# Routing a mixture of experts in two halves: the first among the last causal heads, the second behind the first weighted sums

## The reference

```python
h = _rms(x, n1_w)                                # causal attention, 16 heads of 16
attn = softmax(where(causal, rms(q) @ rms(k).T / 4, -inf))
x = x + (attn @ v @ wo.T with channels 0..63 set to 0)
xf = _rms(x, n2_w)
logits = nan_to_num(xf @ gate_w.T)               # 4 experts
probs = softmax(logits)
topv, topi = top_k(probs, 2)
topv = topv / (topv.sum(-1) + 1e-8)
wts = zeros.at[token, topi].add(topv)
o0 = gelu(xf @ e0_up.T) @ e0_down.T
o1 = silu(xf @ e1_w1.T) * (xf @ e1_w2.T) @ e1_down.T
o2 = gelu(gelu(gelu(xf @ e2_l1.T) @ e2_l2.T) @ e2_l3.T) @ e2_l4.T
o3 = gelu(gelu(xf @ e3_down.T) @ e3_up.T) @ e3_out.T
x = x + (sum of wts[:, e] * oe with channels 0..63 set to 0)
x = layernorm(x)
```

## Time and profile before

| | |
|---|---|
| runs of the kernel, us | 1109.04, 1127.35, 1121.53 |
| median, us | 1121.53 |
| the profiled execution, us | 1125.14 |
| its span, us | 1123.30 |
| its mean granted clock of PE | 0.934 |
| PE busy | 968.8 us (86%) |
| DVE busy | 676.0 us (60%) |
| ACT busy | 591.4 us (53%) |
| POOL busy | 291.2 us (26%) |

### The profile page before, as it was taken

One profiled execution on the slowest core, in us unless ns is written; L12 is line 12 of the kernel. 1 busy time (PEld: TensorE's weight loads), 2 busy tenths in 40 slices (PEclk: granted clock), 3 DMA queues, 4 the chain that ended last, 5 costly groups with the idle time before them and its releaser, 6 DMA issues.

```text
span 1123.3 us, 22133 instructions
## 1 busy us (share of the span) xinstructions
PE 968.8 (86%) x8864; PEld 700.9 (62%) x8864; DVE 676.0 (60%) x1576; ACT 591.4 (53%) x1390; POOL 291.2 (26%) x305
## 2 busy tenths in 40 slices
PE   7997878888779998999898688888888888978997
PEld 4664556666458885566666556666666566645755
DVE  3346545455849965656566477766767766539302
ACT  4632556444348965454554355455546545567444
POOL 3521332000240005212112131221221222337344
PEclk9997899769889999999999899999899899989999
DMA  9350545400668977452252243313213202100001
GB/s 317 106 92 22 122 109 81 116 12 1 204 208 309 315 262 257 151 175 88 96 180 97 71 129 112 104 35 121 77 62 112 56 1 99 71 1 1 1 1 33
DMA packets 66679, 123.72 MB, mean 110 GB/s; under 512 B 11632, under 2 KB 41968, under 8 KB 62496
## 3 DMA queue, kind: packets, MB, share of 16 engines
q1 hardware_dynamic: 64528, 117.48, 34.4%
q0 software_dynamic: 2048, 4.82, 1.4%
HBM read 86.30 MB, written 35.92 MB: 109 GB/s over the span
## 4 chain that ended last, share of the span: by engine, by line
PE 52%; DVE 22%; ACT 12%; DMA 6%; issue 4%; POOL 3%; SPq 1%; POOLq 0%; DVEq 0%; ACTq 0%
PE psum L413 36%; ACT s_p L2803 4%; DVE s_p L2845 3%; DVE s_max L2834 2%; DMA raw_wd<-in_wd 2%; PE psum L2762 2%; PE psum L2773 2%; PE psum L1410 2%; DVE s_pT L2826 1%; PE psum L2236 1%; DVE junk L1930 1%; PE psum L2946 1%; PE psum L568 1%; DVE s_max L687 1%; DMA ctx_raw<-in_ctxT 1%
## 5 line engine op out<-in xcount | busy, mean ns | idle before, releaser
L2803 ACT ACTIVATE s_p<-psum,s_max 112x375 f32<-112x375 f32 x128 | 72.1, 568 | 98.3 <-DVE s_max L2834 98.3
L734 POOL TENSOR_TENSOR rstd<-meanvar,minus_half 112x1 f32<-112x1 f32 x40 | 25.7, 643 | 245.4 <-DVE meanvar L679 172.0
L687 DVE TENSOR_REDUCE s_max<-psum 112x2 f32<-112x750 f32 x64 | 59.5, 936 | 37.5 <-PE psum L568 36.5
L2762 PE MATMUL psum<-ident,s_p 112*125 112x112 f32 x384 | 62.6, 295 | 9.4 <-DVE s_p L2845 4.5
L2834 DVE TENSOR_REDUCE s_max<-psum 112x1 f32<-112x375 f32 x128 | 63.7, 539 | 2.1 <-PE psum L2754 1.9
L2754 PE MATMUL psum<-s_k,s_q 64*112 64x375 f16 x384 | 46.7, 349 | 19.3 <-ACT s_p L2803 7.4
L2762 PEld LDWEIGHTS psum<-ident,s_p 112*125 112x125 f32 x384 | 51.0, 197 | 19.8 <-DVE s_p L2845 6.8
L413 PE MATMUL psum<-Wv,ctx 128*125 128x512 f16 x240 | 59.8, 400 | 3.4 <-issue 2.6
L3200 POOL TENSOR_TENSOR rs<-ms,minus_half 112x32 f32<-112x32 f32 x8 | 43.5, 5437 | 70.8 <-DVE ms L3128 70.8
L413 PE MATMUL psum<-ctx,Wk 128*128 128x375 f16 x320 | 60.6, 324 | 0.0
L1472 ACT ACTIVATE s_pT<-psum 125x672 f32<-125x672 f32 x64 | 46.6, 729 | 22.3 <-PE psum L1398 20.9
(11 more groups left out here) (403 smaller groups left out, 2488.4 us busy)
## 6 DMA issues: line engine op xcount, KB each, us to landing
keys<-s_k SPq DMA_DIRECT2D x64, 187.5 KB, 2.3
s_k<-keys SPq DMA_DIRECT2D x8, 1500.0 KB, 7.7
values<-s_v SPq DMA_DIRECT2D x48, 224.0 KB
s_v<-values SPq DMA_DIRECT2D x16, 672.0 KB
raw_wg<-in_wg SPq DMA_DIRECT2D x8, 1024.0 KB, 6.7
raw_wu<-in_wu SPq DMA_DIRECT2D x8, 1024.0 KB, 7.1
raw_wd<-in_wd SPq DMA_DIRECT2D x8, 1024.0 KB, 7.7
s_kd<-k_halves SPq DMA_DIRECT2D x48, 93.8 KB, 3.8
```

The costliest lines, as they stand in the source:

```text
L687: VE.tensor_reduce(s1_max[b % 2][:, 2 * p:2 * p + 2], rings["s1"][unit][0:N, :, 0:S], X, ALU.max, negate=True).then_inc(*V.up("max1", n))
L2762: ins = TE.transpose(rings["t4"][unit][0:SCH, c * N:(c + 1) * N], p[:, c * SCH:(c + 1) * SCH], ident[0:N, 0:N])
L2803: SC.activation(rings["p4"][2 * n + j], rings["s4"][(n, j)][0:N, 0:S], ACT.Exp, bias=s4_max[b % 2][:, h:h + 1], accum_out=s4_sum[b % 2][:, ...
```

## The change

The routing is made in two halves, each step over four batches instead of eight.

- The routing's tiles are allocated in stage 4 already, at the place in SBUF where stage 6 had them. The functions for the steps (`take_logits`, `scalar_route`, `vector_route`, `route`) move to stage 4's part and take the half `hf`.
- Stage 4's filler places the gate products of batches 0 to 3 first, ahead of all 14 tiles. A new stream, `s5_first_route`, then gives `tp6 0` (two memsets and the copy of the logits), steps 0 to 4 in one round, `exp6 0`, and steps 5 to 21 in four groups, one a round. PE's gate products of batches 4 and up wait for `tp6 0`. The gelus (`la`) are placed only once `exp6 0` is placed.
- In stage 6 `gate6 1` copies the logits of batches 4 to 7 (no memsets), steps 0 to 4 of half 1 come all in the next round instead of one in each of five, `exp6 1` stands where `exp6` stood, and steps 5 to 21 come in four groups behind `ax 0 0 3`, one group a round.
- The folding `ax e hf j` waits for step 21 of its own half. The order of the weighted sums changes: experts 0, 1 and 3 of the first half, `e3_up 1`, `e2_l1 0`, experts 0, 1 and 3 of the second half, `e2_l1 1`, and on as before.
- The splits of `e3_out` and `e2_l1` change places, and those behind them are tied to other units.

```diff
     def s5_ahead():
         yield from until(("out", 4, B - 1), ("xfT5e", 3), ("split5p", FIRST[3], KC - 1))
+        for b in range(4):
+            yield [("gate5", b)]
         for i, at in enumerate(AHEAD):
             yield from until_banks(1)
             yield [("aheadV" if i % 2 else "aheadA", *at)]
-            if 4 <= i < 8:
-                yield [("gate5", i - 4)]
...
+    def s5_first_route():
+        yield from until(("gate5", 3))
+        yield [("tp6", 0)]
+        yield from route_until_exp(0)
+        yield [("exp6", 0)]
+        yield from route_behind_exp(0)
+
+    def route_until_exp(hf):
+        yield [("r6", hf, n) for n in range(5)]
+
+    def route_behind_exp(hf):
+        for some in (range(5, 9), range(9, 13), range(13, 17), range(17, 22)):
+            yield [("r6x8" if n in (8, 9) else "r6", hf, n) for n in some]
+
     def s5_first_gelu():
-        yield from until(("s5e", B - 1, 3))
+        yield from until(("s5e", B - 1, 3), ("exp6", 0))
...
         elif what == "gate5":
             pe.wait_ge(A["oT4", B - 1, 1])
+            if b >= 4:
+                pe.wait_ge(V["tp6", 0])
             gate_product(b, T.up("gate5", b))
...
+    def vector_route(what, hf, n):
+        if n:
+            dve.wait_ge(A["exp6", hf] if n == 5 else V["r6", hf, n - 1])
+        else:
+            dve.wait_ge(V["tp6", hf])
+        if what == "r6":
+            route(hf, n).then_inc(*V.up("r6", hf, n))
+            return
+        for b in range(4 * hf, 4 * hf + 4):
+            ins = VE.max(top5[:, b, :], pr5[:, b, :]) if n == 8 else \
+                VE.max_index(top5_i[:, b, :], top5[:, b, :], pr5[:, b, :])
+            ins.then_inc(*(V.up("r6", hf, n) if b % 4 == 3 else V.up()))
...
     def s6_experts():
         yield from s6_gated()
-        yield from until(("r6", 4))
-        yield [("exp6",)]
+        yield from until(("r6", 1, 4))
+        yield [("exp6", 1)]
         yield from s6_layer("e0_up", 1)
         yield from s6_layer("e3_down", 1)
         yield from s6_layer("e3_up", 0)
-        for e in range(2):
-            for hf in range(2):
-                yield from s6_add(e, hf)
+        for e in (0, 1, 3):
+            yield from s6_add(e, 0)
         yield from s6_layer("e3_up", 1)
-        for hf in range(2):
-            yield from s6_layer("e2_l1", hf)
-            yield from s6_add(3, hf)
+        yield from s6_layer("e2_l1", 0)
+        for e in (0, 1, 3):
+            yield from s6_add(e, 1)
+        yield from s6_layer("e2_l1", 1)
...
     def s6_route():
-        yield [("gate6",)]
-        for n in range(5):
-            yield [("r6", n)]
-        yield from until(("exp6",))
-        for n in range(5, 22):
-            place(("r6x8" if n in (8, 9) else "r6", n))
-            if n % 2:
-                yield None
+        yield [("gate6", 1)]
+        yield from route_until_exp(1)
+        yield from until(("ax", 0, 0, 3))
+        yield from route_behind_exp(1)
...
                 (w16_w, "e0_down", ("gt", 1, 1)), (w16_w, "e1_down", ("gt", 1, 3)),
-                (w16_w, "e2_l1", ("ly", "e3_down", 1, 1)), (w16_w, "e3_out", ("ax", 0, 0, 0)),
-                (w16_w, "e2_l2", ("ax", 0, 0, 3)), (w16_w, "e2_l3", ("ax", 0, 1, 3)),
-                (w16_w, "e2_l4", ("ax", 1, 0, 3))):
+                (w16_w, "e3_out", ("ly", "e3_down", 1, 1)), (w16_w, "e2_l1", ("ax", 0, 0, 3)),
+                (w16_w, "e2_l2", ("ax", 1, 0, 3)), (w16_w, "e2_l3", ("ax", 3, 0, 3)),
+                (w16_w, "e2_l4", ("ax", 0, 1, 3))):
...
                 e, hf, j = at
                 b = hf * 4 + j
                 prior = ORDER.index(e) - 1
-                dve.wait_ge(T["ax", *at], V["r6", 21],
+                dve.wait_ge(T["ax", *at], V["r6", hf, 21],
```

More of the change, by code:

```diff
@@ L2520, in build @@
     step("la", "A gelu, A lh, G ll")
+    step("tp6", "V +2, V tp6")
+    step("r6", "V r6")
+    step("r6x8", "V +3, V r6")
+    step("exp6", "A exp6")
     step("ones5", "V +1, V v1s5, G +3, G mask5")
@@ L2548, in build @@
     UNITS5 = ("ones5", "rms5a", "ms5a", "qkv5", "qkv5e", "ms5", "qk5", "qkT5", "qkT5e", "s5", "mx5", "s5e", "pT5", "av5",
-              "oT5", "turn5", "atT5", "atT5e", "wo5", "sqb5", "msb5", "xf5", "xfT5", "xfT5e", "split5", "aheadA", "aheadV", "split5p", "gate5", "la")
+              "oT5", "turn5", "atT5", "atT5e", "wo5", "sqb5", "msb5", "xf5", "xfT5", "xfT5e", "split5", "aheadA", "aheadV", "split5p", "gate5", "la", "tp6", "r6",
+              "r6x8", "exp6")
     w16_m = Region(nc, work.base, s4_end)
@@ L2734, in build @@
           follow(s5_out, range(1, B, 2)),
-          s5_first_weights(), s5_first_gelu(), filler=ahead_units)
+          s5_first_weights(), s5_first_route(), s5_first_gelu(), filler=ahead_units)
     for units in ahead_units:
-        for unit in units:
+        for unit in units or ():
             place(unit)
@@ L3026, in gpsimd_gelu_low, with take_logits, scalar_route @@
                          ALU.subtract).then_inc(*G.up("ll", name, hf, f))
+    def take_logits(hf):
+        here = slice(4 * hf, 4 * hf + 4)
+        VE.tensor_copy(tp5[:, here], psum[0:N, GATE_BANK, 4 * hf * E1:(4 * hf + 4) * E1].rearrange(
+            "p (b e) -> p b e", e=E1)).then_inc(*V.up("tp6", hf))
+    def scalar_route(hf):
+        here = slice(4 * hf, 4 * hf + 4)
+        act.wait_ge(V["r6", hf, 4])
+        SC.activation(tp5[:, here], lg5[:, here], ACT.Exp).then_inc(*A.up("exp6", hf))
@@ L3107, in scalar_s5 @@
             scalar_first_gelu(*at)
+        elif what == "exp6":
+            scalar_route(*at)
     def vector_s5(what, at, unit):
@@ L3182, in vector_s5 @@
             vector_split5p(*at)
+        elif what == "tp6":
+            VE.memset(pr5[:], -1.0).then_inc(*V.up())
+            VE.memset(cl5[:], 0.0).then_inc(*V.up())
+            dve.wait_ge(T["gate5", 3])
+            take_logits(*at)
+        elif what in ("r6", "r6x8"):
+            vector_route(what, *at)
     def gpsimd_s5(what, at):
@@ L3236, in build @@
     rings.update(up6=banks(0, 4), misc6=Ring([psum[:, i, :] for i in (GATE_BANK, 4, 5, 7)]), raw5=Ring(raw5))
[L3237 to L3240, removed]
+    step("gate6", "T lg6, V tp6", "misc6", "V tp6")
     step("ly", "T ly, A gelu, A lh, G ll", "up6", "A gelu", 1500)
@@ L3283, in s6_add @@
     def s6_add(e, hf):
-        yield from until(("r6", 21), ("split5", ("e0_down", "e1_down", "e2_l4", "e3_out")[e]))
+        yield from until(("r6", hf, 21), ("split5", ("e0_down", "e1_down", "e2_l4", "e3_out")[e]))
         for j in range(4):
@@ L3396, in scalar_s6 @@
             elif what == "exp6":
-                act.wait_ge(V["r6", 4])
-                SC.activation(tp5[:], lg5[:], ACT.Exp).then_inc(*A.up("exp6"))
+                scalar_route(*at)
             elif what == "ly":
@@ L3423, in vector_s6 @@
         fence(dve, 5)
-        mx, den, ts = sm5[:, 0, :], sm5[:, 1, :], sm5[:, 2, :]
         def vector_gated_high(hf, f, raw_):
```

124 lines of the change are left out of this document (59 added, 65 removed).

## The result

The changed kernel took 1127.47 us in the median (1120.64 to 1140.02, 21 runs), the kernel before 1123.85 us beside it (1109.04 to 1135.48, 21 runs). The ratio is 1.0066 [1.0039, 1.0093]: within 2%, but slower by more than the interval. The ratio, some 7 us, is of the fast runs alone (12 of the 21 before, 20 of the 21 after), while the medians of all runs differ by 3.6 us (1.0032). So the sign of the loss is known, and its size not well. The forecast was 5.4 us faster, 1116.2 us in a range of 1105 to 1126; the median lies above that range.

A forecast was written before the change was run, and what follows sets the result against it. PE was taken as the bound (busy 86% of the span, 52% of the chain). Terms -4.27 - 2.09 - 0.3 + 0.7 + 0.6 = -5.4 us took the median 1121.53 to 1116.2 us, range 1105 to 1126.

The forecast's parts named there:

- The gap and the clock behind it: Stage 6's weighted sums: PE's wait for `x_tok` goes, -4.27 us, and the half-speed clock after it, -2.09 us.
- DVE's rounds: Stage 6: DVE's rounds of one folding plus routing steps outlast PE's, stalling PE +0.7 us, bounds 0 and +3.
- Steps 0 to 4 in one round: Stage 6: steps finish before ACT's exponential asks, so it and the gelus come earlier; -0.3 us, bounds 0 and -1.
- Stage 5: Added first-half routing and early gates, mostly covered by DVE's idle time and earlier PE products: +0.6 us, bounds -2 and +6.
- the rival of contention in stage 5: POOL slows 12 routing steps to 1.0 us, block 15.5 us, onto batch 7's chain; net +4.6, 1126; chance 0.07.
- PE reaches `qkT5 6` and `qkv5 7` 1.4 us sooner: Stage 5 cover: gates of 3 x 0.47 us stand before these products where two ahead tiles took 2.44.
- between `xHe 4 7` and the first `mx5 6 0`: Stage 5: all 22 first-half routing steps stand together here on DVE, 5.8 us, where it sat idle 3.20 us.
- The 3.2 us of idle DVE: Stage 5: DVE's wait for PE between 960.67 and 964.78, counted as 3.2 of 5.2 us cover for the routing steps.
- The clock in stage 5: Stage 5's tail: more PE work at low clock can only help, at most 1.5 us; counted as nothing.
- stage 5 gives it back: Routing block of 5.8 us delays `mx5 6 0` and `ms5 7` in full: +3 to +5, net -1.5 to -3.5, 1119; chance 0.16.
- slower: POOL's port contention stretches stage 5's routing block to 15.5 us, 10.3 past its cover; net +4.6, 1126; chance 0.07.

The follow-up runs named there:

- h3: As g2, but routing steps 0 to 4 of batches 4 to 7 given one a round; ratio to the kernel before 0.9984 [0.9940, 1.0029].
- g2: As f1, but the planner counts a gate product at 1150 ns instead of 400; ratio to the kernel before 1.0005 [0.9967, 1.0042].
- g4: The kernel of e3 run again on another chip; ratio to the kernel before 0.9954 [0.9916, 0.9993].
- f3: Changed kernel, gates in old slots, first half's 22 routing steps and `exp6 0` as first units of stage 6; ratio to the kernel before 1.0008.
- g3: Changed kernel with only a gate product's planned cost raised from 400 to 1150 ns; ratio to the kernel before 1.0056 [1.0024, 1.0089].
- f1: Changed kernel, gates still first, first half's routing steps 0 to 21 placed only behind `mx5 7 2`; ratio to the kernel before 1.0055.
- h2: As g3, but steps 0 to 21 and `exp6 0` of the first half in one planner round; ratio to the kernel before 1.0042.
- e1: Changed kernel, gates still first, first half's steps 0 to 21 and `exp6 0` at stage 5's end, gelus not waiting; ratio to the kernel before 1.0025.
- e3: Changed kernel with only the gate products of batches 0 to 3 back in their old slots; ratio to the kernel before 0.9938 [0.9908, 0.9967].
- f2: As f1, but `turn5 5` held back until the norm of batch 7 is placed; ratio to the kernel before 1.0025 [0.9968, 1.0082].
- g1: As e3, but routing steps 0 to 4 of batches 4 to 7 given one a round; ratio to the kernel before 0.9953 [0.9917, 0.9989].
- f4: As e3, but routing steps 5 to 21 of the first half placed behind `turn5 7`; ratio to the kernel before 1.0012 [0.9964, 1.0060].
- e2: As e1, but the gate products of batches 0 to 3 back in their old slots; ratio to the kernel before 1.0011 [0.9975, 1.0046].
- e4: Changed kernel, gates still first, first half's routing steps 0 to 21 placed only behind `ms5 7`; ratio to the kernel before 1.0034.

## Why the prediction was wrong

- *The gap and the clock behind it* (-4.27, -2.09) and *DVE's rounds* (+0.7): right. They add to -5.66; first weighted sum to the end gave 96.04 - 90.23 = -5.81, and -5.7 to -5.8 in every variant. One by one they are off by some tenths that partly cancel: the 192 matmuls took 8.08 + 8.08 us where gap and all took 4.12 + 4.27 + 14.45, so -6.68 for -6.36; the stalls behind them were 0.4 for 0.7; and some 0.5 us were lost elsewhere in the stage, for which there was no term.
- *Steps 0 to 4 in one round* (-0.3): wrong in sign. gt-ax grew by 1.20 us in the change. I looked at ACT's exponential, which comes 1.2 us earlier behind `gt 1 0` (13.56 for 14.76), and not at the evictions of `gt` that DVE makes meanwhile and PE waits for. h3 shows 1.3 us for this edit at equal clocks. One of the five steps took 1.03 us while POOL worked:
```profile
1013.63 1.03 DVE L3096 TENSOR_SCALAR lg<-tp 112x16 f32<-112x16 f32 x1
```
- *Stage 5* (+0.6, bounds -2 and +6): the step that failed; it measured +9.65, beyond the upper bound, and this made the change slower. The durations were right: 22 steps in 5.9 us (forecast 5.8), none stretched, so the rival of contention in stage 5 wasn't it. What failed is "PE reaches `qkT5 6` and `qkv5 7` 1.4 us sooner" (they came 0.6 and 5.2 us later; the figures given for it, 2.44 and 3 x 0.47, also make 1.0 and not 1.4) and the block's place "between `xHe 4 7` and the first `mx5 6 0`". I followed the planner for the units that move and took the order of the others as it was. But the four fillers at 400 instead of 1150 ns move every unit held by a `rest`: `turn5 5` came ahead of the norm of batch 7, `qkv5 7` behind the first scores of batch 6, three ahead tiles before `qkT5 7` instead of one. g2 shows it: with a planned cost of 1150 the gates first cost 53.66 - 52.96 = 0.7 us (against g4) instead of 7.6. The 3.2 us of idle DVE, my main cover, was an idle stretch of the old order.
- *The clock in stage 5* (counted as nothing, and only as a gain): wrong too. Up to `xfT5 7` TensorE ran 4.8 us at the lower level before and 21.4 in the change. Over all kernels the two go together (f3: 3.4 us and 51.89; g3: 23.9 us and 64.44), so the clock is a rival for the whole loss, and no experiment was built to hold it still. The traces bound it: 1.24 us at the norm and 2.7 ahead of `qkT5 7`, 3.9 of the 9.65. The rest is there without it: the norm is 2.94 us late in f1 with no low clock ahead of it, and `ms5 7` 5.1 us late in h2 against g2 with equal low-clock stretches ahead of it. Whether the order brings the low clock isn't shown; that it falls at the same places in kernels with the same order speaks for it.
- The rival "stage 5 gives it back", at +3 to +5 for a block that costs its full length, named the right mechanism for its part (1.6 us at `ms5 7` between the change and e1, 5.1 in h2), but not that of the gates. Its net, -1.5 to -3.5, doesn't follow from its terms, which give -0.7 to -2.7. The rival "slower" had the sign and the size of the sum (+4.6) by luck: its mechanism, steps held up by POOL in stage 5, is not in the change's trace.
- Whole sum: 9.65 + 1.20 - 5.81 = +5.04 us in the profiles; the ratio's interval is 4.4 to 10.4 us.

Two parts of the loss are shown by e3 and g2 (the order) and h2 (the block's length); the clock's part is read from pairs of traces. Not settled is why POOL's power of the same shape takes 6.87 us in the change, e1, f1 and f2, 6.34 in h2 and 5.43 or 5.44 in all others: a subtraction of `e_up` on DVE ran inside it in both groups (it began 0.36 or 0.37 us into the power in the four, 0.14 to 3.88 in the others). Nor why g2 and h3, with the stretches of g4 and g1, have ratios 0.003 to 0.005 higher; the intervals overlap, and by the medians of all runs h3 stands at 0.9973.

## What to carry to other kernels

Where a planner orders the instructions, an edit that moves cheap units changes the place of all that its clock or its filler rule holds back: print the whole order of both and compare it before costing the edit, and let a moved unit count what the unit that it replaces counted. An idle stretch of an engine is cover for new work only if it stays idle in the new order and nothing on the shared path stands behind the work; here nearly the same steps moved the end of stage 5 by 0.7 us (e3), 3.1 (f4) or 6.0 (h2), or the start of stage 6 by 5.1 (e2), by place alone. Work whose result is wanted much later goes into small pieces behind everything that somebody waits for, but inside its stage where the next one waits for all of it.

## What the runs showed of the hardware

- The first low clock came with the gates. In nine of the ten kernels with gates first TensorE falls to its lower level (1.2 of 2.4 GHz) 6.5 to 7.9 us behind `out 4 7`, in none of the seven with gates in old slots, before included. f1, the tenth, has the change's order there and stays at the full clock until 23.4 us, so the gates don't bring it every time. Windows of PE in the change, then in g4: length, busy us, granted clock, DMA share, GB/s.
```profile
945.20:948.20 3.00, 1.47 (x25) 0.98 1.04 415
948.20:955.00 6.80, 6.80 (x33) 0.51 0.65 271
```
```profile
950.70:953.70 3.00, 1.47 (x24) 1.00 1.04 416
953.70:960.50 6.80, 6.21 (x41) 1.00 0.64 265
```
PE was busy for 1.47 of the 3.0 us ahead of both windows. What differs is what it ran then; that this is the cause isn't shown. 12 gate matmuls of 4 columns took 2.13 us in the change, where four take 0.47 at the full clock. g2 has 6.8 us of it from 7.9 us on, and its query product still comes 1.8 us sooner than before.
- Kernels with the same order in stage 5 have their next low-clock stretches at the same places behind `out 4 7`, though each trace is of another execution: at 47.6, 47.4 and 48.5 us in the kernel before, e2 and f3, at 37.3 and 54.4 in e3, 37.0 and 54.1 in g4, 37.9 and 55.0 in g1, at 38.6 and 55.6 in g2 and 38.4 and 55.5 in h3. Their lengths can differ (10.2, 17.1 and 10.2 us in the first three).
- POOL's power of 5.44 us in e4 held none of DVE's steps inside it: those with two inputs in SBUF took 0.17 us.
- A step that needs the shared ports can wait longer than for one instruction: 3.44 us in f4, through four operations of POOL without a pause between them. The Trainium skill (SBUF — State Buffer, "Who interferes with whom") has the loser wait for the whole instruction of the other side; the trace has it wait for the row of them.
